# One batch's row chain dealt out over the attention's second half, and five experts that take batch 0 first

## The chip, the cores and the metric

The kernel runs on one core of a Trainium2 chip. The metric is the device time of one execution in microseconds (us), as the median of several. Engines are called PE (TensorE), PEld (its weight load), DVE (VectorE), ACT (ScalarE), POOL (GpSimd) and SP (SyncE, which only issues transfers).

## The reference

A decoder of two layers, float32, for B = 2 batches of S = 1024 rows, D = 256 wide. Only the first layer matters here; its three blocks are

```python
x = x + attn(layernorm(x))           # 16 heads of 16, 4 key heads, causal, then @ w_o
x = x + xattn(ctx, layernorm(x))     # each row looks at 4 of 77 context rows
x = x + moe(layernorm(x))            # 8 experts, 2 for each row, at most 320 rows of a batch each
# xattn, for a row c:
p      = 77 * sigmoid(V_p @ tanh(W_p @ c))          # a place in the context
window = clip(int(p) - 2 + arange(4), 0, 76)
a      = softmax(ctx[window] @ W_a @ c) * exp(-(window - p)**2 / 2)
# moe: logits = x @ gate.T; the best two; a running count over the batch's rows
# gives each chosen row its place in an expert's table of 320;
# expert e: (silu(rows @ w1[e]) * (rows @ w3[e])) @ w2[e], weighted and added back
```

The second layer (attention with relative positions, another cross attention, another set of experts) is the same before and after.

## The kernel before

One program, one stage after another: `context_prep`, the first attention (`attention0`), the way from its heads through the experts (`middle`), the second attention (`attention1`), and a tail. A stage ends in `end_stage`, a barrier of all engines. Inside a stage every engine runs its own instructions strictly in the order of one list of steps written by the program; it waits on semaphores only, so a step that waits holds back all that stands behind it on that engine. PSUM has 8 banks.

**attention0.** Its list comes from `attention_steps`. Eight groups n (2 batches x 4 key heads) of 12 cells each, numbered c = 12 n + i over all groups, so c = 0 to 95. A cell is 128 keys against up to 512 queries for 4 heads (`r`). For a cell the list has four "key" steps (scores into a PSUM bank, exp by ACT into `pT`), which run one cell ahead; a "value" step, which multiplies `pT` by the values; and between them "row" steps for the next group: PE writes a 128-row score tile, DVE takes its maxima (L760), and PE has two buffers for them. POOL masks the diagonal block of 8 cells in 12 (L747). "key", "turn" (maxima turned) and "heads" (output turned, scaled by DVE) share a ring of three banks: `claim` waits for the job three places back to be emptied. Groups 0 to 3 are batch 0, so its heads are whole once cell 48 has begun; that is at about 281 us, and cells 49 to 69 lie between 284 and 343 us.

**middle.** `middle_order` writes the list. The *row chain* of a group of 512 rows g (0, 1 are batch 0; 2, 3 are batch 1) is: `turn` and `out` (heads @ w_o, added to x), `stat` (mean and variance on DVE, square root on ACT), `shift` (DVE; then ACT normalises the rows into `xn`), `norm` (rows turned by PE), `hid` and `pos` (the place p, tanh on ACT), `mask` (DVE), `score` (PE, DVE, exp on ACT), `sum` (DVE), `flip`, `value`, again `stat`, `shift`, `norm`, then `logit`. For a batch: `best` (the two best experts, DVE), `cum` (running count, PE), `slot` (table indices, DVE), and `scatter`: 16 indirect transfers by POOL into `disp`. POOL also computes `gs` for the score. The list first has both chains (`lead` and `rest`), and only batch 1's last norms, logits, `best`, `cum` and `slot` (`under`) stand between expert steps.

The experts follow as `items` (expert, batches): a *narrow* item is one batch (320 rows), a *wide* one both (640 rows).

```python
items = [(0, (0,)), (1, (0,)), (0, (1,)), (1, (1,))] + [(e, (0, 1)) for e in range(2, E - 2)] + [
    (E - 2, (0,)), (E - 1, (0,)), (E - 2, (1,)), (E - 1, (1,))]
```

An item is `rows` (its rows loaded from `disp` and turned; L1619), seven `ffn` steps (w1 and w3 slices by PE, L1632; silu by ACT, L1725; product into `hT` by DVE, L1928) and `y` (times w2, L1642). PE may be two `ffn` steps ahead of `hT`. SP loads rows and weights; the weights have two buffers, and a pair is refilled when the item that used it last has done its `ffn` (w1, w3) and its `y` (w2). An item's products go by POOL into `ybuf`; for each batch POOL gathers them by index and DVE adds them to x.

Of the kernel before, what the change touches and what calls it, by code (L numbers as in the profile page):

```python
# [10 lines left out]
F32 = mybir.dt.float32  # L11
# [7 lines left out]
P = 128  # L19
B, S, D = 2, 1024, 256  # L20
N = B * S
# [488 lines left out]
def attention_steps(cells, groups, ahead):  # L510
# [33 lines left out]
    return steps  # L544


def attention0(k):
# [4 lines left out]
    tag = "0"  # L552
    with ExitStack() as ctx:
# [27 lines left out]
        steps = attention_steps(cells, G, 8)  # L581
        LD = 16 * 2 * TERMS
        RING = 3
        ring = [s for s in steps if s[0] in ("key", "turn", "heads")]
# [13 lines left out]
        with nc.Block() as block:  # L598
            @block.sync
            def _(sp):  # L600
# [33 lines left out]
                sp.wait_ge(s_fill, 16 * (2 * (E // 2 + 1) + 2))  # L634

            @block.tensor
            def _(pe):
                def claim(x):
                    if x >= RING:
                        kind = ring[x - RING][0]  # L640
                        if kind == "key":
                            pe.wait_ge(s_exp, place("key", x - RING))
                        elif kind == "turn":
                            pe.wait_ge(s_split, 5 * place("turn", x - RING) - 3)
                        else:
                            pe.wait_ge(s_out, place("heads", x - RING))

                rows = job = 0
                for step in steps:
# [36 lines left out]
                    elif step[0] == "heads":  # L686
# [8 lines left out]
                        job += 1  # L695
                    else:
# [16 lines left out]
            def _(act):  # L713
                job = 0
                for step in steps:
# [17 lines left out]
                    job += step[0] in ("key", "turn", "heads")  # L733

            @block.gpsimd
            def _(pool):
# [4 lines left out]
                for n in range(G):  # L741
                    for i, (hq, kb, q0, w) in enumerate(cells):
                        if q0 == kb * P:
# [4 lines left out]
                                                    channel_multiplier=-1, compare_op=ALU.is_ge, fill=nothing).then_inc(s_tri, 1)  # L748

            @block.vector  # L750
            def _(dve):
                nc.vector.memset(zero[:, :], 0.0).then_inc(s_zero, 1)
                rows = job = 0
                for step in steps:
# [40 lines left out]
                    job += step[0] in ("key", "turn", "heads")  # L795
        k.end_stage()
    middle(k, out)
# [501 lines left out]
def middle_order(items):  # L1299

    def two(kind, g):
        return [(kind, g, 0), (kind, g, 1)]

    lead = ([("prep",)] + two("turn", 0) + two("turn", 1) + two("out", 0) + [("stat", 0)] + two("out", 1) + [("shift", 0), ("stat", 1)] +
            two("norm", 0) + [("hid", 0), ("shift", 1), ("pos", 0)] + two("norm", 1) + [("mask", 0), ("score", 0), ("hid", 1), ("pos", 1)] +
            two("turn", 2) + [("mask", 1), ("score", 1), ("sum", 0), ("flip", 0)] + two("out", 2) + [("sum", 1), ("flip", 1)] +
            two("value", 0) + [("stat", 4)] + two("value", 1) + [("stat", 5), ("shift", 4)] + two("turn", 3) + two("norm", 4) +
            [("logit", 0), ("shift", 5)] + two("norm", 5) + [("logit", 1), ("best", 0), ("cum", 0), ("slot", 0)])  # L1310
    rest = (two("out", 3) + [("stat", 2), ("stat", 3), ("shift", 2)] + two("norm", 2) + [("shift", 3), ("hid", 2)] + two("norm", 3) +
            [("pos", 2), ("hid", 3), ("mask", 2), ("score", 2), ("pos", 3), ("mask", 3), ("score", 3), ("sum", 2), ("flip", 2),
             ("sum", 3), ("flip", 3)] + two("value", 2) + [("stat", 6)] + two("value", 3) + [("stat", 7), ("shift", 6)])
    under = (two("norm", 6) + [("shift", 7), ("logit", 2)] + two("norm", 7) + [("logit", 3), ("best", 1), ("cum", 1), ("slot", 1)])
    order = lead + rest + [("rows", 0)]
    for n in range(len(items)):
        for f in range(FC0):
            order.append(("ffn", n, f))
            while under:
                order.append(under.pop(0))  # L1320
                if order[-1][0] not in ("shift", "best"):
                    break
# [1207 lines left out]
```

## Time and profile before

| | us |
|---|---|
| median of 3 runs (1936.18 to 1939.67) | 1938.69 |
| profiled execution: its own time | 1936.54 |
| profiled execution: span | 1934.8 |
| first attention's steps, about | 131 to 410.8 |
| row chains alone, to the first `ffn` | 410.8 to 550.6 |
| experts, to the end of PE's last `y` | 550.6 to 980.4 |

Share of the span that the engines are busy: PE 84%, DVE 54%, ACT 45%, POOL 29%. The share is an average over stages with different limits, so a stage is read by its own window. All times below are from the span's start. The device time is 1.7 us above the span.

### The profile page before, as it was taken

Reading aid. Unit: us, or ns where it says so; the run is one execution under the profiler, and the core shown is the slowest. Engines: PE = TensorE matmul, PEld = TensorE weight load, DVE = VectorE, ACT = ScalarE, POOL = GpSimd, SP = SyncE. Lnnn points to the kernel's source line nnn. Section 1 sums busy time; section 2 is a strip of 40 time slices with the busy share of each in tenths; the row PEclk is TensorE's granted clock in tenths of the full one; section 3 lists DMA queues with packets and bytes.
Section 4 is the critical chain, followed back from the end, with each engine's and each line's share of the span. In section 5 each row is a group of like instructions: output and inputs, shape, how many; then the busy total and the mean of one; then the engine's idle time right before and its main releaser. Section 6 shows DMA issues by size and latency. Waiting matters only on the chain. (4 is left out here: it accounts for less than half of the span.)

```text
span 1934.8 us, 34483 instructions
## 1 busy us (share of the span) xinstructions
PE 1622.1 (84%) x12814; PEld 1092.5 (56%) x12814; DVE 1049.7 (54%) x2134; ACT 875.7 (45%) x1467; POOL 554.9 (29%) x791
## 2 busy tenths in 40 slices
PE   4668899876576999999927819999999999997888
PEld 2323333335454777777713406777777777776644
DVE  4557777624441111111236328888888888884556
ACT  2115666653231111111106108888888887883431
POOL 2201111110303000000333115556555565553011
PEclk9759999987677999999967659999999999998899
DMA  2541121030101232221213286687786886854100
GB/s 82 124 156 22 22 43 22 2 120 1 51 7 64 84 116 85 84 78 54 64 52 129 82 109 194 181 201 200 204 208 193 205 210 193 201 172 157 72 12 33
DMA packets 207560, 207.44 MB, mean 107 GB/s; under 512 B 20612, under 2 KB 186131, under 8 KB 207267
## 3 DMA queue, kind: packets, MB, share of 16 engines
q1 hardware_dynamic: 202531, 191.61, 37.1%
q0 software_dynamic: 4864, 13.64, 2.1%
q8 instruction: 103, 1.69, 0.4%
q14 instruction: 62, 0.51, 0.1%
HBM read 123.18 MB, written 81.81 MB: 106 GB/s over the span
## 5 line engine op out<-in xcount | busy, mean ns | idle before, releaser
L1174 DVE CUSTOM_DVE_ANT_0 prob<-ps,dev 128x1024 f32<-128x1024 f32 x256 | 311.5, 1218 | 30.3 <-DMA dev<-skew_u 27.4
L1072 ACT ACTIVATE prob<-prob,nmax 128x1024 f32<-128x1024 f32 x256 | 293.5, 1146 | 38.4 <-DVE nmax L1174 38.2
L1004 PE MATMUL ps<-cst,prob 128*128 128x128 f32 x2048 | 279.1, 277 | 1.1 <-ACT probT L1079 0.9
L1004 PEld LDWEIGHTS ps<-cst,prob 128*128 128x128 f32 x2048 | 227.3, 141 | 44.0 <-issue 21.6
L1632 PE MATMUL ps<-xeT,w 128*128 128x320 f32 x896 | 246.8, 436 | 5.0 <-ACT xeT L1713 5.0
L723 ACT ACTIVATE pT<-ps 128x512 f32<-128x512 f32 (+3 forms) x384 | 166.1, 495 | 153.3 <-PE ps L683 150.9
L1188 DVE COPY probT<-ps 128x512 f32<-128x512 f32 x256 | 176.3, 689 | 102.9 <-PE ps L1004 102.9
L760 DVE TENSOR_REDUCE nmax<-ps 128x1 f32<-128x128 f32 (+7 forms) x256 | 185.2, 754 | 82.1 <-PE ps L664 80.9
L1632 PEld LDWEIGHTS ps<-xeT,w 128*128 128x128 f32 x896 | 170.1, 191 | 76.9 <-ACT xeT L1713 5.2
L1079 ACT ACTIVATE probT<-ps 128x512 f32<-128x512 f32 x256 | 151.3, 591 | 102.1 <-PE ps L1004 102.1
L1725 ACT ACTIVATE sg<-ps 128x320 f32<-128x320 f32 (+1 forms) x84 | 44.2, 526 | 330.4 <-PE ps L1632 328.7
L987 PE MATMUL ps<-ks,qs 96*128 96x512 bf16 (+4 forms) x768 | 155.7, 312 | 33.5 <-DVE nmax L1174 22.3
L1928 DVE TENSOR_TENSOR hT<-ps,sg 128x320 f32<-128x320 f32 (+1 forms) x84 | 50.6, 603 | 197.6 <-ACT sg L1725 190.9
L1642 PE MATMUL ps<-w,hT 128*128 128x256 f32 (+1 forms) x616 | 140.7, 388 | 5.9 <-DVE hT L1928 5.8
L662 PE MATMUL ps<-ks,qs 96*128 96x512 bf16 (+3 forms) x384 | 111.5, 356 | 38.1 <-DVE nmax L760 25.4
L1045 PE MATMUL ps<-probT,vg 128*18 128x128 f32 (+1 forms) x4096 | 135.9, 273 | 0.0
L1642 PEld LDWEIGHTS ps<-w,hT 128*128 128x128 f32 (+1 forms) x616 | 112.1, 185 | 31.6 <-DVE hT L1928 7.8
L747 POOL TENSOR_SCALAR_AFFINE_SELECT pT<-pT 128x512 f32<-128x512 f32 x64 | 40.8, 637 | 282.9 <-ACT pT L723 282.9
L683 PE MATMUL ps<-qs,ks 99*128 99x512 bf16 (+3 forms) x384 | 110.2, 337 | 13.6 <-ACT pT L723 7.3
L1045 PEld LDWEIGHTS ps<-probT,vg 128*18 128x18 f32 (+1 forms) x4096 | 106.4, 98 | 17.3 <-issue 16.9
L1749 POOL DMA_DIRECT2D ybuf<-ye x32 | 20.5, 644 | 319.6 <-DVE ye L1944 180.8
L1128 POOL TENSOR_TENSOR wm<-wr,cst 128x256 f32<-128x256 f32 x128 | 94.0, 734 | 43.9 <-DMA wr<-skew_p 41.0
(310 smaller groups left out, 2247.9 us busy)
## 6 DMA issues: line engine op xcount, KB each, us to landing
dev<-skew_u SPq DMA_DIRECT2D x128, 256.0 KB, 3.5
skew_p<-prob SPq DMA_DIRECT2D x128, 256.0 KB, 3.3
w<-in_L_ffn_w SPq DMA_DIRECT2D x24, 896.0 KB, 6.3
skew_u<-cst SPq DMA_DIRECT2D x64, 256.0 KB, 4.1
wr<-skew_p SPq DMA_DIRECT2D x128, 128.0 KB, 3.0
qs<-qd SPq DMA_DIRECT2D x96, 128.0 KB, 3.9
ks<-kd SPq DMA_DIRECT2D x48, 256.0 KB, 6.0
qd<-parts SPq DMA_DIRECT2D x48, 128.0 KB, 1.8
```

Source lines behind the costliest of these rows:

```text
L662: last = nc.tensor.matmul(ps[:, bank, 0:hi - lo], query, ks[0:KS, j, lo:hi], start=True, stop=hi < w)
L723: nc.scalar.activation(pT[:, c % 2, r, 0:w], ps[:, ring_bank(job), 0:w], ACT.Exp).then_inc(s_exp, 1)
L760: nc.vector.tensor_reduce(nmax[:, n % 2, r * KB + a:r * KB + a + 1], slot[:, 0:w], AX.X, ALU.max, negate=True).then_inc(s_max, 1)
L987: last = nc.tensor.matmul(ps[:, 2 * (t % 2) + lo // 512, lo % 512:lo % 512 + hi - lo], qs[:, n % 2, r, a * P:(a + 1) * P], ks[:, n % 2, r, ...
L1004: last = nc.tensor.transpose(ps[:, ring_bank(job), kb * P:(kb + 1) * P], prob_tile(t, (4 * h + kb) * P, (4 * h + kb + 1) * P), k.c("ident"))
L1045: last = nc.tensor.matmul(ps[r * VW:r * VW + wide, 7, q % 4 * P:q % 4 * P + P], vg[:, n % 2, r, kb, int(kb == a), 0:wide], probT[:, (HQ * ...
L1072: nc.scalar.activation(prob_tile(t, 0, S), prob_tile(t, 0, S), ACT.Exp, bias=nmax[:, t % 4:t % 4 + 1], scale=-1.0).then_inc(s_exp, 1)
L1079: nc.scalar.activation(probT[:, t % SLOTS, 0:512], ps[:, ring_bank(job), :], ACT.Copy).then_inc(s_evA, 1)
L1174: nc.vector.tensor_tensor_reduce(out=prob_tile(t, 0, S), in0=scores, in1=dev_tile(t), scale=-1.0, scalar=3.0e38, op0=ALU.add, op1=ALU.min, ...
L1188: nc.vector.tensor_copy(probT[:, t % SLOTS, 512:S], ps[:, ring_bank(job), :]).then_inc(s_evD, 1)
L1632: last = nc.tensor.matmul(ps[:, banks(job)[0] + z * wide + h, 0:CAP], w[:, e % 2, c, f * P:(f + 1) * P], xeT[:, c, h * CAP:(h + 1) * CAP], ...
L1642: last = nc.tensor.matmul(ps[0:w, banks(job)[0] + t // 2, t % 2 * D:(t % 2 + 1) * D], hT[:, f, o:o + w], w2[:, e % 2, f, :], start=(f == 0 ...
```

## The change

Three things move.

1. Batch 0's whole row chain and its scatters go into `attention_steps`: from cell 49 on, behind the fourth key step of each cell, and behind the second one of each odd cell while the chain still has work for PE, the next steps are dealt, up to and with one PE job. There are 32 such jobs, so they take the cells 49 to 69; `slot` and the first scatter follow at cell 70 and one scatter in each cell after it. A chain job takes a bank of the ring of three.
2. Batch 1's whole chain goes between the steps of the first four items: one PE job behind each `ffn` and each `y`, again 32, so `cum` stands right behind the `y` of item 3 and `slot` behind the first `ffn` of item 4.
3. Experts 0 to 4 take batch 0 first, then 4 to 0 batch 1; only expert 5 stays wide. Experts 2, 1 and 0 are loaded a second time: 11 sets of weights instead of 8. The first two sets are loaded during the attention.

Both chains use one class, `RowChain`. In it POOL normalises the rows (before: ACT), and ACT empties every `norm` (before: half of them DVE).

```diff
@@ attention_steps
+    under = list(chain)
...
+            if c >= start and (r == 3 or r == 1 and c % 2 == 1 and under and under[0][0] != "scatter"):
+                while under:
+                    steps.append(("chain", under.pop(0)))
+                    if steps[-1][1][0] in RowChain.SINGLE + ("scatter",):
+                        break
@@ attention0
+        chain = RowChain(k, ctx, 0, out, wgt, idx_g)
+        steps = attention_steps(cells, G, 8, chain.order + [("scatter", t, c) for t in range(KB) for c in range(2)], NC * KVH + 1)
...
+                    if n == 1:
+                        chain.load(sp)
+                    if n == KVH:
+                        for e in range(2):
+                            sp.dma_start(w1[:, e, :, :], k.d["L0_ffn_w1"][e].rearrange("(c p) f -> p c f", p=P)).then_inc(s_w, 16)
...
+    SINGLE = ("prep", "turn", "out", "norm", "hid", "pos", "score", "flip", "value", "logit", "cum")
@@ chain_order(b), g = 2 * b, h = g + 1
+    return (two("turn", g) + [("prep",)] + two("out", g) + two("turn", h) + [("stat", g)] + two("out", h) + [("shift", g), ("stat", h)] +
+            two("norm", g) + [("shift", h), ("hid", g)] + two("norm", h) + [("pos", g), ("hid", h), ("mask", g), ("score", g), ("pos", h),
+            ("mask", h), ("score", h), ("sum", g), ("flip", g), ("sum", h), ("flip", h)] + two("value", g) + [("stat", 4 + g)] +
+            two("value", h) + [("shift", 4 + g), ("stat", 4 + h)] + two("norm", 4 + g) + [("shift", 4 + h), ("logit", g)] +
+            two("norm", 4 + h) + [("logit", h), ("best", b), ("cum", b), ("slot", b)])
@@ experts_order
+    def deal():
+        while under:
+            order.append(under.pop(0))
+            if order[-1][0] in RowChain.SINGLE:
+                break
...
         for f in range(FC0):
             order.append(("ffn", n, f))
...
+            deal()
         if n + 1 < len(items):
             order.append(("rows", n + 1))
         order.append(("y", n))
+        deal()
@@ experts
+    AHEAD = 5
+    items = ([(e, (0,)) for e in range(AHEAD)] + [(e, (1,)) for e in reversed(range(AHEAD))] +
+             [(e, (0, 1)) for e in range(AHEAD, E - 2)] + [(E - 2, (0,)), (E - 1, (0,)), (E - 2, (1,)), (E - 1, (1,))])
...
+                    if n == AHEAD:
+                        sp.wait_ge(chain.s_sc, 16 * 2 * KB)
```

PE in the attention, in group 4 (batch 1's first), over one cell. `ks,qs` and `cm` are a row tile, `qs,ks` a key step, `pT,va` the value step. Before:

```order
L683 MATMUL ps<-qs,ks 128x384
L708 MATMUL ps<-pT,va 32x512 x4
L683 MATMUL ps<-qs,ks 128x256
L662 MATMUL ps<-ks,qs 128x256
L664 MATMUL ps<-cm 128x128
L683 MATMUL ps<-qs,ks 128x256
L662 MATMUL ps<-ks,qs 128x512
L662 MATMUL ps<-ks,qs 128x384
L664 MATMUL ps<-cm 128x128
L683 MATMUL ps<-qs,ks 128x256 x2
```

The same place in the change, with its own line numbers:

```order
L712 MATMUL ps<-qs,ks 128x384
L1514 MATMUL ps<-xT_c,wpT 100x512 x2
L745 MATMUL ps<-pT,va 32x512 x4
L712 MATMUL ps<-qs,ks 128x256
L691 MATMUL ps<-ks,qs 128x256
L693 MATMUL ps<-cm 128x128
L712 MATMUL ps<-qs,ks 128x256
L691 MATMUL ps<-ks,qs 128x512
L691 MATMUL ps<-ks,qs 128x384
L693 MATMUL ps<-cm 128x128
L1509 MATMUL ps<-cst,xn_c 128x128 x4
L712 MATMUL ps<-qs,ks 128x256 x2
```

`hid` of rows 0 to 511 (L1514) now stands behind a fourth key step, and a `norm` (L1509) behind a second one.

ACT in the attention a little earlier, at the chain's first two `stat` steps. Before it holds nothing but `pT<-ps` (L723) and `oT<-ps` there. In the change (L760 is the exp of a key step, L1554 and L1565 empty a `turn` and a `norm`, L1558 is the square root):

```order
L1554 ACTIVATE turned_c<-ps 128x2x2x128
L760 ACTIVATE pT<-ps 128x256 x2
L1558 ACT_TABLE_LOAD
L1558 ACTIVATE rstd_c<-rstd_c 128x4
L760 ACT_TABLE_LOAD
L760 ACTIVATE pT<-ps 128x128 x4
L760 ACTIVATE pT<-ps 128x512 x2
L1558 ACT_TABLE_LOAD
L1558 ACTIVATE rstd_c<-rstd_c 128x4
L1565 ACTIVATE xT_c<-ps 128x2x2x128
L760 ACT_TABLE_LOAD
L760 ACTIVATE pT<-ps 128x512 x2
```

Each square root now has a table load ahead of it and one behind it; there are 8 loads of this kind in the attention, and 15 in the experts' stage, where the silu of the experts (L1955) is the other table. Before, the attention has none past its first, and the middle 10.

DVE at the end of batch 1's second `score` (L1859 to L1861) and its two `sum` steps (L1867 to L1871). Before, `sum` follows at once:

```order
L1859 TENSOR_TENSOR x_sc<-ps,x_tmp 128x308
L1860 TENSOR_REDUCE x_mx<-x_sc 128x4
L1861 TENSOR_TENSOR x_sc<-x_sc,x_mx 128x308
L1867 TENSOR_TENSOR x_sc<-x_sc,x_cnt 128x308
L1868 TENSOR_REDUCE x_sm<-x_sc 128x4
L1870 TENSOR_TENSOR x_sc<-x_sc,x_gs 128x308
L1871 RECIPROCAL x_sm<-x_sm 128x4
```

In the change the `hT` product of an expert slice (L2011) stands between them:

```order
L1681 TENSOR_TENSOR x_sc_c<-ps,x_tmp_c 128x308
L1682 TENSOR_REDUCE x_mx_c<-x_sc_c 128x4
L1683 TENSOR_TENSOR x_sc_c<-x_sc_c,x_mx_c 128x308
L2011 TENSOR_TENSOR hT<-ps,sg 128x320
L1689 TENSOR_TENSOR x_sc_c<-x_sc_c,x_cnt_c 128x308
L1690 TENSOR_REDUCE x_sm_c<-x_sc_c 128x4
L1692 TENSOR_TENSOR x_sc_c<-x_sc_c,x_gs_c 128x308
L1693 RECIPROCAL x_sm_c<-x_sm_c 128x4
L2011 TENSOR_TENSOR hT<-ps,sg 128x320
```

## Rows read from the trace of the kernel before

**Rows 1.** The page: the span of the profiled execution, and the row maxima of the attention.

```profile
span 1934.8 us, 34483 instructions
...
L760 DVE TENSOR_REDUCE nmax<-ps 128x1 f32<-128x128 f32 (+7 forms) x256 | 185.2, 754 | 82.1 <-PE ps L664 80.9
```

**Rows 2.** Windows: length, busy us (count) by engine, granted clock, DMA share, GB/s.

```profile
284.00:343.00 59.00, 53.13 (x397) 21.27 (x393) 43.93 (x80) 36.30 (x84) 8.92 (x14) 1.00 0.12 20
...
410.80:550.60 139.80, 86.53 (x361) 67.79 (x361) 66.14 (x233) 42.15 (x81) 21.38 (x24) 0.68 0.18 62
550.60:980.40 429.80, 404.20 (x1658) 300.77 (x1658) 78.97 (x156) 62.34 (x120) 50.12 (x62) 0.97 0.21 71
```

**Rows 3.** Timeline of PE, 410 to 560 us: start, length, engine, line, tiles, count, wait.

```profile
415.27 0.38 PE L1526 MATMUL ps<-cst,gate 8*128 8x8 f32 x2 [5.40 <-DMA gate<-in_L_ffn_gate_w]
...
550.58 4.08 PE L1632 MATMUL ps<-xeT,w 128*128 128x320 f32 x8 [5.00 <-ACT xeT L1713]
554.50 0.60 PE L1553 MATMUL ps<-cst,xn_nat 128*128 128x128 f32 x4
```

**Rows 4.** Timeline of ACT and DVE behind one expert slice of PE.

```profile
554.70 0.44 ACT L1725 ACTIVATE sg<-ps 128x320 f32<-128x320 f32 x1 [2.87 <-PE ps L1632]
...
555.17 0.49 DVE L1928 TENSOR_TENSOR hT<-ps,sg 128x320 f32<-128x320 f32 x1 [7.39 <-ACT sg L1725]
```

**Rows 5.** Timeline of PE: one wide item and one narrow item of the experts.

```profile
735.26 30.31 PE L1632 MATMUL ps<-xeT,w 128*128 128x320 f32 x112
...
782.50 17.93 PE L1632 MATMUL ps<-xeT,w 128*128 128x320 f32 x66
...
902.73 15.34 PE L1632 MATMUL ps<-xeT,w 128*128 128x320 f32 x56
...
928.60 15.34 PE L1632 MATMUL ps<-xeT,w 128*128 128x320 f32 x56
```

**Rows 6.** Timeline of PE: jobs of a row chain at full clock.

```profile
463.08 3.62 PE L1590 MATMUL ps<-ctxn,aT 77*128 77x256 f32 x16
...
515.03 1.93 PE L1561 MATMUL ps<-xT,wpT 128*100 128x512 f32 x4
...
559.68 1.85 PE L1601 MATMUL ps<-gateT,xT 128*128 128x8 f32 x16
...
577.57 2.82 PE L1610 MATMUL ps<-r_cand,cst 128*128 128x56 f32 x14
```

**Rows 7.** Timeline of DVE: mask and score, sum, and best, each its first and last.

```profile
439.20 0.16 DVE L1841 TENSOR_SCALAR x_pt<-x_pt 128x4 f32<-128x4 f32 x1
...
444.25 0.48 DVE L1861 TENSOR_TENSOR x_sc<-x_sc,x_mx 128x308 f32<-128x308 f32 x1
...
452.70 0.47 DVE L1867 TENSOR_TENSOR x_sc<-x_sc,x_cnt 128x308 f32<-128x308 f32 x1
...
453.72 0.48 DVE L1870 TENSOR_TENSOR x_sc<-x_sc,x_gs 128x308 f32<-128x308 f32 x1
...
573.83 0.21 DVE L1788 TENSOR_REDUCE r_m<-r_lg 128x8 f32<-128x64 f32 x1
...
577.01 0.22 DVE L1893 TENSOR_TENSOR r_cand<-r_oh 128x64 f32<-128x64 f32 x1
```

**Rows 8.** Timeline of ACT in the tail: a table load between two that are ready.

```profile
1821.49 0.63 ACT L2321 ACTIVATE sg<-g 128x512 f32<-128x512 f32 x1 [3.41 <-DVE g L2349]
1822.13 1.28 ACT L2311 ACT_TABLE_LOAD   x1
1823.47 0.46 ACT L2311 ACTIVATE xsc<-xsc 128x308 f32<-128x308 f32 x1
```

**Rows 9.** Waits of PE, 550.6 to 980.4 us: total, times, longest.

```profile
PE ps L1619 <- DMA xe<-disp: 15.3, 1, 15.3
...
PE ps L1607 <- DVE r_cand L1893: 4.4, 1, 4.4
```

**Rows 10.** Lines of POOL, 0 to 60 us: busy, mean ns, idle before.

```profile
L215 POOL TENSOR_SCALAR x<-x,inv0a,shift0a 128x256 f32<-128x256 f32 x16 | 8.8, 560 | 28.3 <-ACT xs0a L202 28.3
```

More of the change, by code:

```diff
@@ L794, in _ @@
                         last.then_inc(s_out, 1)
-                    job += step[0] in ("key", "turn", "heads")
+                    elif step[0] == "chain":
+                        chain.vector(dve, link, step[1], ps[:, ring_bank(job), :])
+                    job += on_ring(step)
         k.end_stage()
-    middle(k, out)
+    experts(k, out, wgt, idx_g, (w1, w3, w2))
 def attention1(k):
@@ L1296, in _, with chain_order @@
                 nc.vector.tensor_copy(k.relk[:, 0:1], ps[0:KS, 4, P:P + 1]).then_inc(s_rel, 1)
-def middle_order(items):
+def chain_order(b):
     def two(kind, g):
         return [(kind, g, 0), (kind, g, 1)]
[L1306 to L1315, printed above, removed]
@@ L1325, in middle_order, with experts @@
         order.append(("y", n))
+        deal()
+    assert not under
     return order
-def middle(k, heads):
+def experts(k, heads, wgt, idx_g, weights):
     nc, ps, x = k.nc, k.ps, k.x
-    ROWS = 2 * CAP
-    GT = 4
-    items = [(0, (0,)), (1, (0,)), (0, (1,)), (1, (1,))] + [(e, (0, 1)) for e in range(2, E - 2)] + [
-        (E - 2, (0,)), (E - 1, (0,)), (E - 2, (1,)), (E - 1, (1,))]
-    order = middle_order(items)
-    SINGLE = ("prep", "turn", "out", "norm", "hid", "pos", "score", "flip", "value", "logit", "cum")
-    jobs = [s for s in order if s[0] in SINGLE + ("rows", "ffn", "y")]
-    where = {s: i for i, s in enumerate(jobs)}
-    lead = where[("rows", 0)]
-    def banks(i):
-        kind = jobs[i][0]
-        if kind in SINGLE:
-            return [i % 8] if i < lead else [4 + sum(s[0] in SINGLE for s in jobs[lead:i]) % 4]
-        n = jobs[i][1]
-        side = sum(s[0] not in SINGLE for s in jobs[:i]) % 2
-        first = (2 if n < 4 else 4) * side
-        return list(range(first, first + 2 * len(items[n][1])))
-    def tenants(i):
-        return sorted({max(had) for b in banks(i) if (had := [j for j in range(i) if b in banks(j)])})
-    def place(i):
-        return sum(s[0] == jobs[i][0] and (s[0] != "norm" or s[2] == jobs[i][2]) for s in jobs[:i + 1])
-    def done(step):
-        return where[step] + 1
-    normed = [s[1] for s in order if s[0] == "shift"]
-    summed = [s[1] for s in order if s[0] == "stat"]
-    tiles = [[(o, min(P, CAP * len(h) - o)) for o in range(0, CAP * len(h), P)] for _, h in items]
-    final = {e: max(n for n, it in enumerate(items) if it[0] == e) for e in range(E)}
-    ybuf = [k.nc.dram_tensor(f"ybuf{b}", (E * CAP, D), F32, kind="Internal").ap() for b in range(B)]
-    disp = k.disp
@@ L1401, in middle @@
+        own = [s for s in jobs if s[0] not in RowChain.SINGLE]
+        split = max(n for n in range(len(items)) if ("ffn", n, 0) in jobs[:where[("cum", 1)]]) + 1
+        assert split <= AHEAD
         xe = k.sb("xe", [P, ST, D], ctx=ctx)
```

954 lines of the change are left out of this document (507 added, 447 removed).

## The prediction

> **What bounds the kernel now.** I read the page first, then the windows of the stages that the change touches, then timelines inside them.
>
> The span is 1934.8 us, the profiled execution's own time 1936.5 [rows 1]. The sum is made against 1936.5; the median of the runs shown, 1938.7, is 0.1% above it, less than the 0.2% (about 4 us) that a measurement of this kernel can tell from no change.
>
> From 284 to 343 us, where batch 0's chain is to go, PE is busy 53.1 of 59.0 us, DVE 43.9, ACT 36.3, POOL 8.9, at full clock [rows 2]. PE bounds it closely, and DVE has less room than it seems: its maxima take 0.75 us each in the mean [rows 1], PE may be two of them ahead, and both run in the order of the list.
>
> From 410.8 to 550.6 us PE is busy 86.5 of 139.8 us at a clock of 0.68 [rows 2]: a chain of small steps from engine to engine. That is the stretch to be won.
>
> From 550.6 to 980.4 us PE is busy 404.2 of 429.8 us [rows 2]. A wide item takes 47.24 us from its first `ffn` to the next item's, a narrow one 25.87 [rows 5]. Four wide and eight narrow make 395.9. PE waits 15.3 us for batch 1's scattered rows and 4.4 us for `best` [rows 9]. Four `norm`, two `logit` and `cum` add about 9.3 [rows 3, 6]. Sum 424.9; the other 4.9 us are half-speed stretches behind waits, as at 550.58, where a slice takes 4.08 us instead of 15.34 / 7 = 2.19 [rows 3, 5].
>
> **What PE pays for one chain.** At full clock: 8 `norm` of 0.60 are 4.8 [rows 3]; two `hid` of 1.93, four `value` in 3.62, two `logit` of 1.85, `cum` 2.82 plus its first matmul, about 3.2 [rows 6]; two `score`, sixteen instructions each like `logit`, 3.8; four `out`, 32 instructions of 256 columns at `value`'s 0.226 each, 7.2. Turns, flips, prep and pos are estimated at 5.8, the first two like `norm`. Sum 36 us. In the lead the same work ran at a mixed clock between waits; in either new place PE is kept near full clock by other work.
>
> **Batch 1's chain among the experts.** PE is the bound there, so nothing hides the jobs: 36 us are added. PE also stands where a job needs what DVE does in the same deal, because DVE first waits for the slice just before it. A slice is through silu and `hT` 1.0 us behind PE's end (554.66 to 555.66) [rows 4]. The waits by that:
> - the first `norm` behind a `shift`, twice: 1.0 + 0.4 for `shift` + two tiles on POOL at 0.56 [rows 10] + hand-overs, 2.7 each;
> - first `flip`: from the end of item 2's first slice PE has score, slice, pos, slice, score, slice ahead, and comes to `flip` after 11.6 us. DVE must do `hT` (1.0), mask and score (439.20 to 444.73, 5.5 [rows 7]), ACT exp, table load and silu, DVE two `hT` (9.9 us by now), the second mask and score (15.4), ACT again (17.2), the fourth `hT` (18.2), and `sum`, 1.5 us [rows 7]: 19.7. PE waits 8.1;
> - second `flip`: 1.0 + 1.5, 2.5;
> - `cum`: behind `y`, DVE copies `y` (1.1) and does `best`, 3.4 [rows 7]: 4.7.
>
> Sum 20.7. What is queued behind the waiting PE is the next slice, so ACT and DVE run dry too.
>
> The wait for scattered rows stays 15.3: from `slot` to the rows' turn the same 16 scatters run, and PE again has six slices and no more in between; moved behind the first `ffn` of item 4, it is the same distance as today. POOL's stores stand behind the scatters as before.
>
> Start of the stage: today the first PE job waits until 415.27, 4.5 us behind the last heads, for a transfer [rows 3]. The first rows are two more transfers behind it, then are turned and emptied: 8.8 us by estimate, half of it the transfer. Fourteen narrow and one wide item are 409.4. Half-speed stretches: 7 instead of 4.9, for one more long wait. Together 8.8 + 409.4 + 36 + 20.7 + 15.3 + 7 = 497.2, against 139.8 + 429.8 = 569.6: **72.4 us less**. Three more pairs of narrow items are in it: 2 x 25.87 - 47.24 = 4.5 us each, 13.5.
>
> Three more sets of weights: a set's w1 and w3 are issued at the end of an item's seventh `ffn`. All but one have a whole item as cover. Expert 2's second load has only the `y` and the rows ahead of item 7, 25.87 - 15.34 = 10.5 us [rows 5]. The share of the transfer engines in this stage is 0.21 [rows 2], so I take 0; without the cover it would be a few us, once.
>
> **Batch 0's chain in the attention.** 21 cells carry the 32 jobs. PE adds 36 us. DVE adds about 37: two masks and scores 11, two sums 3, `best` 3.4 [rows 7], and the rest (four `stat`, adds, shifts, `slot`) about 20, since 66.1 us were busy in the lead for not quite two chains [rows 2]. 43.9 + 37 = 81 us stay below PE's 53.1 + 36 = 89, so PE stays the bound, but the long DVE steps stall it. With 0.7 us for a maximum in progress:
> - mask and score, twice: DVE is away 0.7 + 5.5 and needs 0.75 for the next maximum; PE has about 4 us (the score and two row tiles with their keys): 3.0 each;
> - `flip`, twice: 0.7 + 1.5 + hand-over, 2.4 each;
> - `norm` behind `shift` in the same deal, twice: 0.7 + 0.4 + 1.1 + hand-over, 2.5 each;
> - `cum`: 0.7 + 3.4 + hand-over, 4.2;
> - four `stat`, two later `norm`, `slot`: 5.7 together. In a `stat` ACT loads a table, waits for DVE, loads again, and no exp passes.
>
> Sum 25.7. Against that PE's own idle time there, 59.0 - 53.1 = 5.9 us, is filled by chain jobs; I take 4 back. **57.7 us more**; bounds 30 (36 less 5.9: every stall hidden by the ring) and 83 (stalls twice as long). I take the middle, since the waits follow from the order of the lists. The cells from 70 on carry `slot` and scatters; POOL has 8.9 of 59 us busy there and takes them at no cost. Weights loaded in the attention meet a transfer share of 0.12 [rows 2]: no cost. If the first rows were late, the whole would shift by that.
>
> **Sum.** 1936.5 - 72.4 + 57.7 = 1921.8.
>
> A switch of tables is priced from the trace: silu ends at 1822.12, the load takes 1.28 us, and exp begins at 1823.47 [rows 8]: 1.35 us in all. The Trainium skill (ScalarE: Activation LUTs, What ACT_TABLE_LOAD costs) states about 1.28 us for the load and 1.38 us more for a drain, 2.66 for each switch; by that the attention's 8 loads cost 11 us more and the two on the way to the first `flip` 3 more, and the sum would be 1935. The row does not show the drain.
>
> **The rivals.**
> - *Stalls hidden.* The ring of three and the two row buffers give PE more to do than I count. For it: one chain's jobs come in two halves that alternate. Against it: the deal's own waits (`norm`, `flip`, `cum`) have nothing between. 1936.5 - 72.4 + 30 to 45 = 1894 to 1909. Chance 0.15.
> - *DVE becomes the bound of the attention: slower than before.* Long DVE steps delay maxima, the maxima PE, PE's keys ACT, and ACT's squares and exps the next chain step; stalls then add up instead of overlapping. For it: 81 us of DVE work that is queued in strict order, with a wait of DVE for itself between its small steps. It decides from a stretch of 59 + 72 = 131 us on, where I expect 117. With stalls doubled: 1936.5 - 72.4 + 83 = 1947. Chance 0.2.
> - *Each table load drains ACT's queue* of exps and the ring stands: 8 x 1.35 us more on the path and as much among the experts, 1934 to 1939, no change. This is also what the skill's 2.66 would give. Chance 0.08.
> - *The split experts cost more than 4.5 us each*, because the reloaded weights of item 7 come late or PE falls to half speed behind each chain wait: 1930 to 1945. Chance 0.07.
> - The forecast, 1910 to 1934: 0.5.
>
> **How the numbers follow.** The likeliest is 1922. The range takes in the stretch's bounds, 1896 to 1948, and leaves out 2 in 10. Faster by over 0.2% (below about 1933): 0.5 and 0.15 and a little of the others, 0.66. Within 0.2%: 0.12. Slower: 0.22.
>
> **What would show it.** Cells 49 to 69 take about 117 us with PE busy about 89; the first attention ends at about 468 instead of 410.8. The first `ffn` starts about 9 us behind it. PE's waits in the experts' stage: about 15 us for `xe`, 8 for the first `flip`, 4.7 for `cum`. No wait on `w` above 2 us. The prediction is wrong if the attention's end is past 485 (DVE-bound) or before 455, if the first rows are not there, or if the experts' stage, from its start to PE's last `y`, is not 480 to 497 us.

## The result: 0.24% slower than before

The changed kernel takes 1942.18 us in the median of 20 runs (1938.26 to 1947.94), the kernel before 1937.37 us in 20 runs beside them (1934.65 to 1942.37). The ratio is 1.0024, with a 95% interval of 1.0015 to 1.0032. I forecast 1922 us, so the direction was wrong; the measured time lies in the range. The profiled execution of the changed kernel took 1943.75 us itself, with a span of 1942.0.

| stage, in the profiled executions | before, us | after, us | difference | forecast |
|---|---|---|---|---|
| start to the last heads of the first attention | 410.8 | 484.6 | +73.8 | +57.7 |
| from there to the end of PE's last `y` | 569.6 | 498.2 | -71.4 | -72.4 |
| the rest, whose code is the same | 954.4 | 959.2 | +4.8 | 0 |
| span | 1934.8 | 1942.0 | +7.2 | -14.7 |

So the middle came out as forecast. The attention did not.

### The profile after

The page, to set beside [rows 1]: the row maxima cost VectorE what they did, but it stands longer in front of them.

```profile
span 1942.0 us, 34704 instructions
...
L809 DVE TENSOR_REDUCE nmax<-ps 128x1 f32<-128x128 f32 (+7 forms) x256 | 185.7, 754 | 106.9 <-PE ps L693 105.8
```

Windows of the kernel after: the attention from 280 us to its end, and the experts (columns as in [rows 2]).

```profile
280.00:484.30 204.30, 165.85 (x1040) 78.74 (x1038) 109.15 (x280) 106.54 (x233) 47.53 (x68) 0.87 0.17 46
...
492.80:982.80 490.00, 448.80 (x1852) 327.39 (x1852) 109.64 (x280) 90.49 (x176) 61.73 (x82) 0.95 0.24 80
```

The same attention work in the kernel before, a window not shown so far:

```profile
280.00:410.60 130.60, 114.29 (x831) 42.51 (x829) 75.16 (x148) 83.84 (x198) 20.39 (x32) 0.99 0.09 14
```

This pair of windows holds the error. The stretch grows by 73.7 us: PE's busy time by 165.85 - 114.29 = 51.6 us, its idle time from 16.3 to 38.5, by 22.1 us. I had forecast 36 of work, 25.7 of stalls less 4 filled, so 21.7 idle. The idle time agrees (how far by luck is said below). The busy time is 15.6 us too long, and the granted clock says why: it was 0.99 in this stretch before and is 0.87 now, while DVE is busy for no more than 109 of 204 us.

Timeline of the kernel after, inside the chain: start, length, engine, line, tiles, count, and in brackets the wait ahead of it.

```profile
341.22 0.48 DVE L1683 TENSOR_TENSOR x_sc_c<-x_sc_c,x_mx_c 128x308 f32<-128x308 f32 x1
341.73 0.46 ACT L1578 ACTIVATE x_sc_c<-x_sc_c 128x308 f32<-128x308 f32 x1 [3.25 <-DVE x_sc_c L1683]
342.10 0.58 ACT L769 ACTIVATE oT<-ps 128x512 f32<-128x512 f32 x1
342.73 1.11 PE L721 MATMUL ps<-cst,oT 128*128 128x128 f32 x4 [3.91 <-ACT oT L769]
...
347.40 1.93 PE L745 MATMUL ps<-pT,va 128*32 128x512 f32 x8
...
350.52 3.64 PE L1522 MATMUL ps<-gT,xT_c 128*128 128x77 f32 x16
...
359.86 1.14 PE L1526 MATMUL ps<-cst,x_sc_c 128*77 128x128 f32 x4 [3.56 <-DVE x_sc_c L1692]
360.92 1.94 PE L745 MATMUL ps<-pT,va 128*32 128x512 f32 x8
...
368.89 1.14 PE L1526 MATMUL ps<-cst,x_sc_c 128*77 128x128 f32 x4 [2.30 <-DVE x_sc_c L1692]
369.96 1.94 PE L745 MATMUL ps<-pT,va 128*32 128x512 f32 x8
...
376.44 1.06 PE L745 MATMUL ps<-pT,va 128*32 128x512 f32 x8
```

To be seen: DVE does mask and score, ACT stands for it with the exps and `oT` behind, and PE waits 3.91 us for `oT`. Behind that wait the same value step (L745) takes 1.93 us instead of the 1.06 of 376.44; `score` takes 3.64 where I had priced 1.9. That is the chip's 1.2 GHz in place of 2.4: the granted clock is 0.50 from 343 to 373 us, the longer jobs take nearly double, and the waits of 3.56 and 2.30 us lie inside this stretch.

```profile
343.00:373.00 30.00, 24.14 (x95) 12.18 (x95) 14.86 (x39) 8.81 (x18) 1.41 (x2) 0.50 0.08 10
```

The clock had fallen once before, at about 318 us, and there no wait is longer than 1.15 us: PE waits 1.15, 0.60, 0.83 and 0.75 us from 311.9 to 318.4, and then `hid` takes 3.67 us in place of 1.93 [rows 6].

```profile
313.06 0.66 PE L1509 MATMUL ps<-cst,xn_c 128*128 128x128 f32 x4 [1.15 <-POOL xn_c L1598]
...
321.48 3.67 PE L1514 MATMUL ps<-xT_c,wpT 128*100 128x512 f32 x4
```

Waits of PE in the kernel after, 280 to 490 us, and in the experts' stage (as [rows 9]).

```profile
PE ps L1526 <- DVE x_sc_c L1692: 5.9, 2, 3.6
PE ps L721 <- ACT oT L769: 5.9, 4, 3.9
PE ps L1538 <- DVE r_cand_c L1712: 4.1, 1, 4.1
PE ps L1509 <- POOL xn_c L1598: 3.8, 2, 2.7
```

```profile
PE ps L1904 <- DMA xe<-disp: 14.8, 1, 14.8
PE ps L1526 <- DVE x_sc_c L1692: 10.3, 2, 7.8
...
PE ps L1509 <- POOL xn_c L1598: 5.1, 2, 2.5
PE ps L1538 <- DVE r_cand_c L1712: 4.4, 1, 4.4
```

In both stages those that I had priced come close: `flip` 5.9 for 4.8, `cum` 4.1 for 4.2, the first norms 3.8 for 5.0; and among the experts 10.3 for 10.6, 4.4 for 4.7, 5.1 for 5.4, 14.8 for 15.3.

Start of the experts' stage, timeline (to set beside 415.27 in [rows 3]):

```profile
487.11 5.74 SPq L1867 DMA_DIRECT2D xe<-disp  x4
490.39 1.52 PE L1904 MATMUL ps<-cst,xe 128*128 128x128 f32 x6 [6.81 <-DMA xe<-disp]
...
492.77 1.97 PE L1917 MATMUL ps<-xeT,w 128*128 128x320 f32 x3 [0.86 <-ACT xeT L1943]
```

The load of the first rows is issued at 487.11 us, PE turns them from 490.39 on, and the first `ffn` stands at 492.8, 8.2 us behind the last heads.

### The profile page after: what moved, and what is told of

Its sections match the earlier page's. It is cut to its first block and busy times, and to the rows that moved or that the text cites. A ratio compares the mean times of both kernels' runs of the same rounds, so it can differ in the third digit from the quotient of the medians.

```text
span 1942.0 us, 34704 instructions
## 1 busy us (share of the span) xinstructions
PE 1637.4 (84%) x12864; PEld 1090.8 (56%) x12864; DVE 1050.2 (54%) x2159; ACT 885.2 (46%) x1480; POOL 571.1 (29%) x823
## 5 line engine op out<-in xcount | busy, mean ns | idle before, releaser
L1917 PE MATMUL ps<-xeT,w 128*128 128x320 f32 x896 | 260.3, 449 | 1.4 <-ACT xeT L1943 0.9
L760 ACT ACTIVATE pT<-ps 128x512 f32<-128x512 f32 (+3 forms) x384 | 167.0, 495 | 169.2 <-PE ps L712 165.6
L1917 PEld LDWEIGHTS ps<-xeT,w 128*128 128x128 f32 x896 | 174.3, 197 | 75.8 <-issue 11.7
L1955 ACT ACTIVATE sg<-ps 128x320 f32<-128x320 f32 (+1 forms) x105 | 47.7, 455 | 307.1 <-PE ps L1917 299.3
L2011 DVE TENSOR_TENSOR hT<-ps,sg 128x320 f32<-128x320 f32 (+1 forms) x105 | 53.9, 514 | 221.1 <-ACT sg L1955 214.5
L1928 PE MATMUL ps<-w,hT 128*128 128x256 f32 (+1 forms) x658 | 148.7, 384 | 6.1 <-DVE hT L2011 6.0
L691 PE MATMUL ps<-ks,qs 96*128 96x512 bf16 (+3 forms) x384 | 115.5, 368 | 35.7 <-DVE nmax L809 23.3
L1096 PEld LDWEIGHTS ps<-probT,vg 128*18 128x18 f32 (+1 forms) x4096 | 106.6, 98 | 18.3 <-issue 17.8
L1185 POOL TENSOR_TENSOR cst<-wm 128x64 f32<-128x64 f32 x128 | 40.9, 320 | 216.0 <-DVE wr L1243 210.9
```

Of the source, the lines that this page charges most:

```text
L691: last = nc.tensor.matmul(ps[:, bank, 0:hi - lo], query, ks[0:KS, j, lo:hi], start=True, stop=hi < w)
L760: nc.scalar.activation(pT[:, c % 2, r, 0:w], ps[:, ring_bank(job), 0:w], ACT.Exp).then_inc(s_exp, 1)
L1096: last = nc.tensor.matmul(ps[r * VW:r * VW + wide, 7, q % 4 * P:q % 4 * P + P], vg[:, n % 2, r, kb, int(kb == a), 0:wide], probT[:, (HQ * ...
L1917: last = nc.tensor.matmul(ps[:, a + z * wide + h, 0:CAP], w[:, j, c, f * P:(f + 1) * P], xeT[:, c, h * CAP:(h + 1) * CAP], start=(c == 0), ...
L1928: last = nc.tensor.matmul(ps[0:w, a + t // 2, t % 2 * D:(t % 2 + 1) * D], hT[:, f, o:o + w], w2[:, j, f, :], start=(f == 0), stop=(f == FC ...
```

## The experiments

Theory 1: waits of 2 to 4 us are priced rightly, but TensorE falls to half its clock behind them and the doubled jobs are on the path. Rivals: 2, VectorE's and ScalarE's strict order is the path and the clock only follows; 3, ScalarE's table loads; 4, the weights' transfers in the attention. All ratios are to the kernel before; the changed kernel is at 1.0024 (1.0015 to 1.0032). `FILL`, `AHEAD`, `SINGLE` and the steps are the names of the program. Windows, timelines and waits come from one profiled execution each. How far such a one can move is shown by ahead6, whose attention is word for word the changed kernel's: its window from 280 us to the end is

```profile
280.00:487.90 207.90, 170.82 (x1041) 81.80 (x1039) 109.19 (x280) 107.07 (x233) 47.71 (x68) 0.84 0.16 46
```

So without any change to its program the stretch ended at 484.3 or at 487.9 us, with 165.85 or 170.82 us of busy time at a clock of 0.87 or 0.84. This is by itself a sign that the clock is on the path: 5.0 us more of busy time, 3.6 us more of stretch.

### fill: TensorE kept busy in its waits

```diff
+ FILL = {"norm": 24, "flip": 30, "cum": 36, "heads": 30}   # 256 columns each, before the job's own wait
+ many = FILL.get(step[1][0], 0) if len(step[1]) < 3 or step[1][2] == 0 else 0
+ if many:
+     claim(job)
+     fill(job, many)     # matmuls of a constant into the job's own bank
  chain.inputs_ready(pe, step[1])
```

> The changed kernel with matmuls that nobody reads put in front of TensorE's waiting chain jobs in the attention (24 of 256 columns before a group's first norm, 30 before flip and before the heads that follow a score, 36 before cum): the waits for VectorE, ScalarE and GpSimd stay, but TensorE is busy in them. The fillers' rows are bf16 and should take about 0.11 us each at full clock. Theory 1 (the waits of 2 to 4 us take TensorE to 1.2 GHz, and the 15.6 us more busy time than my 36 are the doubled jobs behind them): the granted clock of the attention from 280 us to its end rises from 0.87 to over 0.95, score goes from up to 3.64 us back to 1.9, and the attention ends at 470 to 478 us instead of 484.6; the whole is 7 to 14 us faster than the changed kernel (1928 to 1935). Theory 2 (VectorE's strict order is the bound, the clock only follows): the waits grow by what the doubled jobs lose, the attention ends at 482 to 488, the whole stays at 1940 to 1946. Theory 3 (table loads) and 4 (the weights' transfers in the attention) expect no change either.

Ratio 1.0029 (1.0017 to 1.0042): no gain. Windows of its attention, then the timeline at the first `flip`:

```profile
280.00:485.30 205.30, 176.06 (x1259) 94.31 (x1256) 107.88 (x279) 105.89 (x231) 47.63 (x68) 0.96 0.16 46
```

```profile
359.24 6.29 PE L680 MATMUL ps<-cm 128*128 128x256 bf16 x30 [3.35 <-DVE x_sc_c L1698]
```

The clock rose to 0.96, and the attention still ended at 485.3 us, no earlier. By its total that speaks for theory 2. But the row shows that the test was a bad one. L1698 is the step at whose end the program calls the score's bank free (the last to read the bank is L1696, two steps before): the claim in front of the fillers waits 3.35 us for it, because `flip` stands three places behind `score` on the ring. The fillers start only then, at half clock, and take 6.29 us where 2.6 us were left to cover. All 222 are busy for 31.1 us (their group's row in the list by line) in place of some 24 (222 at the expected 0.11). Fillers that reach past a wait cost what they give.

### fill2: fewer fillers, sized to the waits

```diff
- FILL = {"norm": 24, "flip": 30, "cum": 36, "heads": 30}
+ FILL = {"norm": 8, "flip": 16, "cum": 30, "heads": 30}
```

> As the first kernel with fillers, but with fewer of them, so that they lie inside waits that the profile of the changed kernel shows (8 before a group's first norm, which waits 1.2 and 2.7 us; 16 before flip, of whose 3.6 us about 2.6 are behind the score's read; 30 before cum and before the heads that follow a score, 4.1 and 3.9 us). In the first one the clock rose to 0.96 and the rows of jobs took 13 us less, but the fillers' own 23 us reached past the waits. Theory 1 (the fall of the clock is on the path): with about 13 us of fillers, nearly all covered, the clock of the attention is over 0.93, its end comes 7 to 12 us earlier (473 to 478), the whole 1930 to 1936. Theory 2 (the order in which VectorE and ScalarE are asked is on the path, the clock only follows): the jobs' gain turns up as longer waits again; the end at 483 to 487, the whole 1940 to 1945.

Ratio 0.9995 (0.9983 to 1.0007): 0.29% or 5.6 us faster than the changed kernel, and the two intervals do not touch, with more work on TensorE and VectorE's and ScalarE's order as it was.

```profile
280.00:478.40 198.40, 168.45 (x1157) 84.65 (x1155) 107.56 (x276) 105.36 (x230) 47.53 (x68) 0.94 0.16 47
```

```profile
341.38 4.75 PE L680 MATMUL ps<-cm 128*128 128x256 bf16 x30 [2.94 <-DVE x_sc_c L1698]
341.72 0.58 ACT L784 ACTIVATE oT<-ps 128x512 f32<-128x512 f32 x1
...
345.96 0.60 PE L731 MATMUL ps<-cst,oT 128*128 128x128 f32 x4
...
356.69 2.64 PE L680 MATMUL ps<-cm 128*128 128x256 bf16 x16 [3.36 <-DVE x_sc_c L1698]
...
359.57 1.14 PE L1541 MATMUL ps<-cst,x_sc_c 128*77 128x128 f32 x4 [0.23 <-DVE x_sc_c L1707]
360.63 1.29 PE L760 MATMUL ps<-pT,va 128*32 128x512 f32 x8
```

Now 2.64 us of fillers lie inside `flip`'s wait, of which 0.23 us is left, and the value step behind it takes 1.29 instead of 1.94 us. The attention ended 5.9 us earlier, a little under the 7 to 12 that theory 1 expected. The added matmuls can help only through the clock, so the clock is on the path.

Not all of it comes back, though, for two reasons. The thirty fillers before the heads were too many: `oT` was there at 342.3, the fillers ran until the heads began at 345.96, so 3.6 us of them reached past their wait. What the full clock gave back behind them, from the heads to the row tile ahead of the second `mask` (4.3 us for the 7.7 of the changed kernel), only made up for that. And theory 2 has a part: from that `mask` to `flip` VectorE's order sets the time. `mask` begins at 350.95 us (351.24 in the changed kernel) and `flip` at 359.57 (359.86), 8.6 us later in both, although `score` took 1.96 us for 3.64 and PE came to `flip` at 353.3 instead of 356.3 us. There the half clock had cost nothing. The fillers as a group, in the list by line (busy us, mean ns, idle ahead):

```profile
L680 PE MATMUL ps<-cm 128*128 128x256 bf16 x124 | 17.8, 305 | 6.3 <-DVE x_sc_c L1698 6.3
```

Without their 17.8 us PE is busy for 150.65 of the 168.45, 15.2 less than in the changed kernel, as good as the whole 15.6; but its idle time of 29.95 and the 17.8 are 47.75 against 38.45, so 9.3 us of the gain did not arrive. By my estimate 3.6 of these are the fillers past the heads' wait, and the other 5.7 turned up as waits for other engines, which the slower jobs had hidden before.

### stall: the waits alone, in the kernel before

```diff
+ if step[0] == "key" and step[3] == 2 and (c := NC * step[1] + step[2]) >= 50 and c <= 70 and c % 3 == 2:
+     for z in range(16):
+         nc.vector.tensor_scalar(idle[:, (z + 1) % 2, :], idle[:, z % 2, :], 1.0, 0.0, ALU.mult, ALU.add).then_inc(s_long, 1)
+         longs += 1
+         dve.wait_ge(s_long, longs + 1)
```

> The kernel before with nothing moved; only VectorE gets seven blocks of 16 small linked operations that nobody needs (128x308, about 0.35 us from one to the next, 5.6 us a block, as long as mask and score), in every third cell from 50 to 68 of the attention. TensorE gets no work. By the sum of my prediction a block costs TensorE 3.0 us (0.7 of a maximum in progress, the block, 0.75 for the next maximum, less 4 us that TensorE has to do), 21 in all. If the waits alone were the price: 18 to 24 us slower than before, 1956 to 1961, TensorE's busy time in this stretch as before. Theory 1 (the clock falls behind such waits and the jobs behind them take double): the granted clock of the stretch falls below 0.9, busy time grows by 5 to 12 us, and the whole is 26 to 36 us slower, 1964 to 1974.

Ratio 1.0238 (1.0224 to 1.0252): 46 us slower, beyond every expectation. Window of the attention, and the timeline of the first block:

```profile
280.00:456.40 176.40, 130.47 (x827) 47.17 (x825) 112.11 (x259) 83.93 (x197) 20.36 (x32) 0.86 0.07 10
```

```profile
284.69 5.64 DVE L761 TENSOR_SCALAR idle<-idle 128x308 f32<-128x308 f32 x16
...
291.38 0.71 PE L664 MATMUL ps<-ks,qs 96*128 96x512 bf16 x2 [4.79 <-DVE nmax L769]
291.89 0.31 PE L666 MATMUL ps<-cm 128*128 128x128 bf16 x1
...
294.62 1.94 PE L710 MATMUL ps<-pT,va 128*32 128x512 f32 x8
...
297.90 0.22 PE L666 MATMUL ps<-cm 128*128 128x128 bf16 x1
```

TensorE has no more to do than before, and yet its busy time grows by 130.47 - 114.29 = 16.2 us. After a wait of 4.79 us the masks' matmul (L666) takes 0.31 instead of 0.22 us and the value step 1.94, until 297.9. The other 29.6 us are idle time, 4.2 us a block where I had priced 3.0: TensorE had 1.9 us of work left when the block held the maxima, not 4. So a block of 5.6 us costs 6.5, of which 2.3 by the clock. Here, where TensorE bounds the stretch and nothing is moved, the clock's price comes on top of the wait's.

### spread, late and both of these: smaller portions

```diff
- if c >= start and (r == 3 or r == 1 and c % 2 == 1 and under and under[0][0] != "scatter"):
+ if c >= start and (r == 3 or r == 1 and under and under[0][0] != "scatter"):
      while under:
          steps.append(("chain", under.pop(0)))
-         if steps[-1][1][0] in RowChain.SINGLE + ("scatter",):
+         if steps[-1][1][0] in RowChain.SINGLE + ("scatter", "mask", "sum", "best", "shift"):
```

and, for ScalarE, its part of a step put off to the chain's next step:

```diff
+ if owed:
+     chain.scalar(act, owed, None)
+ owed = step[1] if step[1][0] in ("stat", "score", "best") else None
+ if not owed:
      chain.scalar(act, step[1], ps[:, ring_bank(job), :])
```

Both edits together (spread_late):

> The changed kernel with batch 0's chain dealt in smaller portions, one at every first and third key tile of a cell, where mask, sum, best and shift end a portion of their own (41 portions instead of 32), and with ScalarE's part of stat, score and best moved to the chain's next step, so that it doesn't hold the exps while VectorE works. Theory 1 (waits make the clock fall): waits between jobs shrink below 1 us, the clock stays over 0.95 from 280 us on, the attention ends at 462 to 472 us, the whole is 12 to 22 us faster than the changed kernel (1920 to 1930). Theory 2 (VectorE's total work in order is the bound): VectorE has the same 109 us to do, the end moves by under 5 us, 1937 to 1943. Theory 3 (the 8 table loads cost): they stay, so 8 x 1.3 = 10 us of the loss stay and the gain is under 8 us.

Ratio 0.9930 (0.9909 to 0.9951). The second edit alone (late):

> The changed kernel, and of the smaller portions' kernel only ScalarE's part: its work of stat, score and best is asked for at the chain's next step, the portions are as in the changed kernel. Together the two parts gave 17 us. Theory A (ScalarE's wait for VectorE inside a portion holds the exps and TensorE behind them, as the 3.9 us before the heads at 342.7 show): 5 to 10 us faster than the changed kernel, 1932 to 1937; the wait before the heads is gone. Theory B (it is VectorE's long steps in the same portion as their reader): under 3 us, 1939 to 1943.

Ratio 1.0043 (1.0027 to 1.0058): no gain, so theory A, as an edit, falls. But the wait before the heads, which was to be gone, is not. It has another name, the score's bank on the ring of three, and is 3.0 us long in place of 3.9 (waits of PE, 280 to 490 us):

```profile
PE ps L721 <- DVE x_sc_c L1688: 3.0, 1, 3.0
```

So ScalarE's hold was only the later of two waits at the same place, and late does not show what a shorter hold would be worth alone. The first edit alone (spread):

> The changed kernel with the smaller portions alone (41 portions, mask, sum, best and shift end one of their own, a portion at every first and third key tile), ScalarE's part as in the changed kernel. Theory B (VectorE's long steps in one portion with the TensorE job that reads them): 10 to 17 us faster than the changed kernel, 1925 to 1932. Theory A: 5 to 8 us.

Ratio 0.9934 (0.9916 to 0.9952): 0.90% or 17 us faster than the changed kernel, all of the gain. Window of its attention:

```profile
280.00:465.50 185.50, 154.56 (x1037) 72.40 (x1036) 108.41 (x278) 105.36 (x232) 47.44 (x68) 0.94 0.18 51
```

VectorE does the same 108 us, so its amount of work was never the bound. What counts is how its steps are dealt: its long steps no longer stand in one portion with the TensorE job that reads them, and there is a portion at two places of every cell. The two come together in this edit, and no run separates them. With a few key and row steps in between, `flip` waits 1.8 us for 5.9 in all, `cum` 1.3 for 4.1, TensorE's idle time falls from 38.5 to 30.9 us and, with a clock of 0.94, its busy time from 165.85 to 154.56. The attention ends at 465.5, before the 468 that I had forecast for the change itself. (both, best41 and best37 have the same attention and ended it between 465.3 and 468.4 us, at clocks of 0.90 to 0.94.)

### notable: no table loads

```diff
- self.rstd[:, self.slots(step[1])], ACT.Sqrt).then_inc(self.s_sd, 1)
+ self.rstd[:, self.slots(step[1])], ACT.Sqrt if self.b else ACT.Copy).then_inc(self.s_sd, 1)
```

> The changed kernel with a copy in place of the square root in batch 0's chain (the square root is left out, so rstd is 1 / (var + eps)): the step stays, its 8 table loads in the attention (10.2 us of ScalarE, four in sqrt and four in exp) go. Theory 3 (each load holds the exps and so the ring): 8 to 12 us faster than the changed kernel, 1930 to 1934. Theory 1: the loads stand in only two of the clock's falls; 1 to 4 us faster. Theory 2: the same.

This kernel leaves out batch 0's square roots; its values differ, its steps do not. Ratio 0.9987 (0.9974 to 1.0000): 0.37% or 7 us faster than the changed kernel by the medians; the attention of its profile ends 4.2 us earlier, hardly more than the 3.6 between two profiles of the same attention.

```profile
280.00:480.10 200.10, 163.12 (x1053) 78.69 (x1051) 109.36 (x280) 97.48 (x227) 47.54 (x68) 0.88 0.18 48
```

The eight loads do cost: by the medians 7 us, up to 0.9 us each, less than theory 3's 8 to 12 us and more than theory 1 left for them. The clock, 0.88, is as low as without the edit, so it is a second, smaller cause. It was in my sum only inside the "5.7 together". The Trainium skill (ScalarE: Activation LUTs, What ACT_TABLE_LOAD costs) has 2.66 us for a switch. An estimate from that page is 8 x 2.66 = 21 us for all eight gone; this run shows 7, less even than the 10.2 us that the loads themselves last.

### early: the weights' transfers elsewhere

```diff
- if n == KVH:
+ if n == 1:
      for e in range(2):
          sp.dma_start(w1[:, e, :, :], ...
```

> The changed kernel with the six weight transfers (5.4 MB) of experts 0 and 1 issued behind the first batch's second head group instead of at the chain's start, so that the burst of 325 to 342 us (transfer share above 1) lies far ahead of the chain. Theory 4 (the burst disturbs the chain or the next queries' transfers, and starts the stretch at half clock): the clock of 342 to 400 us rises from 0.68 to over 0.9 and the whole is 8 to 15 us faster. Theories 1 to 3: within 3 us of the changed kernel, 1939 to 1945.

Ratio 1.0034 (1.0020 to 1.0049), and the clock of its attention is no better (0.84, as in ahead6 with the transfers in their old place): theory 4 falls.

```profile
280.00:487.70 207.70, 170.49 (x1040) 81.59 (x1038) 108.88 (x280) 106.67 (x232) 47.55 (x68) 0.84 0.09 19
```

### ahead6, both, best41, best37: the other stage, and what beats both kernels

```diff
- AHEAD = 5
+ AHEAD = 6
```

> The changed kernel with six experts' narrow items of batch 0 ahead of batch 1's instead of five, so that all sixteen items are narrow and batch 1's first rows are wanted one item (25.9 us) later. A sixth pair costs 2 x 25.87 - 47.24 = 4.5 us; the wait of 14.8 us for batch 1's scattered rows should vanish, the waits of the chain stay. If the scatters are what the wait is for: 10 us faster than the changed kernel, 1931 to 1934. If something else (the stores or the weights behind it in the same queues) holds the rows: 4 to 6 us slower, 1946 to 1948.

Ratio 0.9965 (0.9952 to 0.9978): 0.59% or 11 us faster than the changed kernel. Batch 1's wait for its scattered rows is gone; what is left on `xe` is the start of the stage. So its distance from `slot` was worth an item, and the sixth split pair cost about 4 us: from the last heads to PE's last `y` the stage is some 10.5 us shorter, with a wait of 14.8 us gone. With spread (both):

> The changed kernel with the smaller portions in the attention (ratio to before 0.9934) and with six experts' narrow items of batch 0 ahead (0.9965); the changed kernel itself is at 1.0024. The two lie in different stages, so they should add: 1.0024 - 0.0090 - 0.0059 = 0.9875, some 1913 us. If the six experts' gain needs the late start of the stage it would be less.

Ratio 0.9873 (0.9853 to 0.9893): they add. Then the chain among the experts in smaller portions too:

```diff
- if order[-1][0] in RowChain.SINGLE:
+ if order[-1][0] in RowChain.SINGLE + ("mask", "sum", "best", "shift"):   # best41; best37 without "shift"
```

> Both of them, and among the experts batch 1's chain is dealt in the same smaller portions (41 over 48 places). In the changed kernel TensorE waits there 10.3 us for flip, 5.1 for the first norms and 4.4 for cum. Waits theory: these fall to under 5 us together, and the scatters come 9 places (about 20 us) later, which eats most of the item's distance that the sixth expert gave: the wait for scattered rows is back with 0 to 10 us. 8 to 15 us faster than with both alone, less that wait: 1900 to 1910. Rival (the waits among the experts move to other jobs, as TensorE is the bound there): within 3 us of both alone.

> As the one before, but shift doesn't end a portion among the experts (37 portions): the four waits for the first norm stay (5.1 us in the two that wait), the scatters come 4 places (about 9 us) earlier. If the wait for scattered rows had come back with 41 portions, this is faster than it by 0 to 5 us; if not, slower by 3 to 5 us.

best41 is at 0.9852 (0.9836 to 0.9868), which can't be told from both; best37 is at 0.9812 (0.9797 to 0.9827), clear of either. Waits of PE among the experts, best41 and then best37 (the 6.8 us of best37 is the start of the stage, which the 17.6 of best41 leaves out):

```profile
PE ps L1904 <- DMA xe<-disp: 17.6, 1, 17.6
...
PE ps L1538 <- DVE r_cand_c L1712: 2.1, 1, 2.1
...
PE ps L1526 <- DVE x_sc_c L1692: 0.5, 2, 0.3
```

```profile
PE ps L1904 <- DMA xe<-disp: 6.8, 1, 6.8
...
PE ps L1509 <- POOL xn_c L1598: 5.1, 2, 2.5
PE ps L1917 <- DVE hT L2011: 3.8, 2, 3.3
PE ps L1526 <- DVE x_sc_c L1692: 2.4, 2, 2.2
PE ps L1538 <- DVE r_cand_c L1712: 2.2, 1, 2.2
```

With 41 portions `flip` waits almost nothing, but the scatters come too late and 17.6 us on `xe` are back. With 37 `flip` and `cum` still fall from 14.7 to 4.6 us and the rows are there in time. best37, at 1901.42 us (1897.04 to 1904.03), is 1.9% faster than the kernel before.

## Why the prediction was wrong

**The middle, right.** -71.4 us for -72.4: first `ffn` 8.2 us behind the heads (8.8), and the waits as listed above. The splitting of experts cost what I had priced at 4.5 us each (about 4 by ahead6), and no wait on weights shows. The half-speed stretches are there, as at 536.29 us, where a slice takes 4.01 instead of 2.3 us.

**The attention's stalls, right in sum, in part by luck.** 22.1 us of idle time for 21.7. Single items moved: `mask` and `score` don't stall the row tiles (PE's waits for `nmax` are 4.9 us after, 7.0 before) but hold the heads, through ScalarE and through the bank of the score (3.91 us). And I had priced the waits at full clock, while part of this stretch ran at half, where longer jobs hide some of a wait. In fill2, with the clock mostly kept, idle time and the fillers inside waits are 47.75 - 3.6 = 44.1 us, 27.8 more than before the change. So at full clock I was some 6 us too low; this is an estimate from one profile.

**The step that failed** is "in either new place PE is kept near full clock by other work", and with it a sum for the attention that has work and waits but no term for the clock, though the middle's sum has one ("Half-speed stretches: 7"). What was missing is 15.6 us of busy time: the granted clock went from 0.99 to 0.87, behind waits of 2 to 4 us and once behind four of about 1 us. fill2 shows that the clock is on the path (5.6 us back, with the order of the other engines left in place), stall that it costs this without any added work. spread shows that the portions, not VectorE's total, were behind the long stretch. That is shown. How much of the 15.6 was on the path is not settled: fill2 gives 5.9 us, and some 9.5 with the 3.6 of fillers past their wait; the rest was hidden by waits for VectorE, as ahead of the first `flip`. In spread, where the waits are shorter too, 11.3 us of busy time and 7.5 us of idle time went; in the profiles of both and best37, with the same attention, 5 to 6 and 10 to 12. So how the gain of the smaller portions divides into clock and waits is not settled either. The 36 us for the chain's work itself were right: without the fillers, fill2's attention has 150.65 - 114.29 = 36.4 us more than before. So of the 16 us that the attention took beyond the forecast, I put 9 or 10 down to the clock and 6 to waits, by estimate.

**The rivals.** "DVE becomes the bound", priced at 1947, was right in its direction and not in its mechanism: VectorE is idle for 95 of 204 us, the waits for maxima did not grow, and spread took 17 us away with VectorE's work unchanged. What is true in it is the strict order of VectorE's steps. "Each table load drains ACT's queue" (1934 to 1939) is a part: some 7 us by notable. "The split experts cost more" (1930 to 1945) took in the measured time and is wrong, as the middle shows. With 15.6 us more the sum would have been 1937, no change.

**The range and the signs.** That the measured time lies in the range is no merit of the mechanism. Its ends don't follow from the bounds either: 30 and 83 us give 1894 and 1947, not 1896 and 1948. Of my signs of being wrong, the attention's end at 484.6 us stayed just inside its limit of 485. The other limit, 480 to 497 us for the experts' stage, was set badly: from the last heads the stage took 498.2, outside it, but my own 497.2 was outside as well; from the first `ffn` it took 490.0.

**The rest.** Behind the last `y` nothing is changed, but its profile took 959.2 us against 954.4. Of the twelve experiments, whose code there is the same too, this stretch took between 954.4 (best37) and 961.4 us (notable). So single executions differ by that much. But the two profiles of the kernel before, its own and stall's, have 954.4 and 954.7 us, and of the twelve with the changed code eleven have 955.9 or more. So some of the 4.8 us may well belong to the change; how much, and why, stays open.

## What to carry to other kernels

When work is dealt into a stage that TensorE bounds closely, price each wait twice: its length, and the doubled jobs behind it; in stall a wait of 4.2 us cost 2.3 more by the clock. Don't put a long VectorE step in the same portion as the TensorE job that reads it (spread), and count the ring: a job may wait for the bank of the job three places back before it waits for its own input (fill). Spreading a chain pays until what comes out of it is late, so look at who waits for its end (best41 against best37).

## What the hardware showed that I had not expected

One wait of 4.79 us is enough to bring TensorE from 2.4 to 1.2 GHz (value step 1.94 for 1.06 us), and it was back at full rate 6.5 us after it had started again (291.38 to 297.90). In the changed kernel, with waits of 3.91, 3.56 and 2.30 us following each other, it stayed at the lower level for about 30 us. Long waits are not needed: it also fell behind four of 1.15, 0.60, 0.83 and 0.75 us (`hid` 3.67 for 1.93 us). Matmuls of which nothing is used, put in such waits, made the kernel faster (fill2), and too many of them did not (fill).
